# A transformer-like layer chain on one core: the routers' logits are formed inside both attentions, the norm of the routing moves to Pool and ACT

## The reference

```
x = x + conv(group_norm(x));  x = x + box3x3(group_norm(x))
t = tokens(x)                                   # 16 images x 256 tokens of 128 channels
t = t + softmax_attention(ln(t), 8 heads)       # image by image in the kernel
t = t + moe(ln(t), 8 experts, top 2, width 256)     # "d"
t = t + linear_attention(ln(t), 8 heads)
t = t + moe(ln(t), 8 experts, top 2, width 512)     # "f"

def moe(x):                                     # both layers
    logits = x @ router                         # 4096 tokens x 8 experts
    top2, index = top_k(logits, 2);  w = softmax(top2)
    y = sum over the two chosen experts of w * (silu(x @ g[e]) * (x @ u[e])) @ down[e]
```

## Time and profile before

| what | value |
| --- | --- |
| median of 3 runs | 883.47 us (879.12, 883.47, 885.61) |
| the profiled execution | 884.63 us, span in the trace 882.9 us |
| mean granted PE clock | .89 of full speed |
| busy in the span | PE 717.3 us (81%), DVE 521.0 (59%), ACT 416.2 (47%), POOL 401.1 (45%) |
| softmax_attention | to about 302.7 us |
| route d | 302.75 to 365 us |
| linear_attention | about 490 to 596.4 us |
| route f | 596.44 to 651.8 us |

### The profile page before, as it was taken

The page is one execution under the profiler, slowest core; times in us unless marked ns, Lnnn a source line. Parts: engine busy times, 40 slices in busy tenths (PEclk is TensorE's granted clock), DMA queues, the critical chain, the costliest instruction groups (busy, mean ns, idle before and its releaser), DMA issues. The chain is left out here.

```text
span 882.9 us, 17711 instructions
## 1 busy us (share of the span) xinstructions
PE 717.3 (81%) x5093; PEld 560.7 (64%) x5093; DVE 521.0 (59%) x1467; ACT 416.2 (47%) x1075; POOL 401.1 (45%) x436
## 2 busy tenths in 40 slices
PE   3996879899998762988999156568389999999996
PEld 1555656666665462757888145557268888888882
DVE  7447857777776358665555258885863333333334
ACT  2423436767675331565555255544244444444434
POOL 0003245556663033345664577700036676766740
PEclk9997969999998765699999688886569999999999
DMA  3001000000000051164333122205001111111118
GB/s 102 1 1 25 1 1 1 1 0 0 0 1 1 18 186 36 44 186 118 91 89 78 53 55 52 53 4 191 1 21 40 44 47 46 46 49 42 49 29 285
DMA packets 33974, 46.18 MB, mean 52 GB/s; under 512 B 8195, under 2 KB 22663, under 8 KB 33648
## 3 DMA queue, kind: packets, MB, share of 16 engines
q1 hardware_dynamic: 25040, 27.57, 9.8%
q0 software_dynamic: 8864, 17.72, 7.7%
HBM read 30.11 MB, written 15.60 MB: 52 GB/s over the span
## 5 line engine op out<-in xcount | busy, mean ns | idle before, releaser
L1986 DVE TENSOR_TENSOR f_h<-ps,f_silu 128x512 f32<-128x512 f32 x71 | 49.1, 692 | 121.5 <-ACT f_silu L1944 121.5
L1044 DVE TENSOR_REDUCE negmax<-ps 128x2 f32<-128x512 f32 x128 | 82.6, 687 | 44.3 <-PE ps L878 43.4
L1832 POOL DMA_INDIRECT f_xg<-f_normed,f_gather x71 | 68.9, 971 | 78.1 <-POOLq L1469 54.8
L1832 POOL DMA_INDIRECT d_xg<-d_normed,d_gather x71 | 67.6, 952 | 71.0 <-PE ps L1873 42.3
L1944 ACT ACTIVATE f_silu<-ps 128x512 f32<-128x512 f32 x71 | 42.4, 598 | 108.8 <-PE ps L1883 108.8
L1838 POOL DMA_INDIRECT f_results<-f_y,f_scatter x71 | 71.9, 1012 | 45.7 <-issue 32.0
L785 ACT ACTIVATE prob<-ps 128x512 f32<-128x512 f32 x128 | 69.6, 598 | 42.2 <-PE ps L897 42.1
L1262 POOL DMA_INDIRECT e_yg<-d_results,d_slot_u x64 | 61.5, 961 | 32.4 <-issue 18.6
L1904 PE MATMUL ps<-f_w_out,f_hT 128*128 x568 | 75.2, 276 | 0.6 <-DVE f_y L1992 0.6
L1904 PEld LDWEIGHTS ps<-f_w_out,f_hT 128*128 128x128 f32 x568 | 69.0, 192 | 0.9 <-issue 0.8
L1986 DVE TENSOR_TENSOR d_h<-ps,d_silu 128x256 f32<-128x256 f32 x71 | 30.0, 423 | 37.5 <-ACT d_silu L1944 36.7
(11 more groups left out here) (357 smaller groups left out, 1956.2 us busy)
## 6 DMA issues: line engine op xcount, KB each, us to landing
d_results<-d_y SPq DMA_DIRECT2D x71, 64.0 KB, 1.8
f_raw<-in_f_in SPq DMA_DIRECT2D x16, 256.0 KB, 3.0
f_ys<-f_results SPq DMA_DIRECT2D x8, 512.0 KB, 6.7
X<-in_x SPq DMA_DIRECT2D x4, 512.0 KB, 5.4
d_normed<-X SPq DMA_DIRECT2D x8, 256.0 KB, 2.0
d_raw<-in_d_in SPq DMA_DIRECT2D x8, 256.0 KB, 2.7
f_normed<-X SPq DMA_DIRECT2D x8, 256.0 KB, 2.0
f_w_out<-in_f_out SPq DMA_DIRECT2D x1, 2048.0 KB, 8.7
```

What stands on the lines that cost most here:

```text
L1044: nc.vector.tensor_reduce(negmax[:, :, h // HG, col:col + 1], ps[:, 2 + h % 2, :].rearrange("p (t k) -> p t k", t=2), AX_X, ALU.max, negat ...
L1832: nc.gpsimd.indirect_dma_start(xg[:, n % 4, :], None, moe.xn_dram, bass.IndirectOffsetOnAxis(ap=moe.gather[:, n:n + 1], axis=0)).then_inc( ...
L1986: nc.vector.tensor_tensor(h[:, n % 2, :], UP(n), silu[:, n % 2, :], ALU.mult).then_inc(h_ready, 1)
```

## The change

The logits of a normalised token are (t @ r - mean x sum(r)) / deviation. With a router whose column means are taken off, the mean falls out, and the factor 1/deviation doesn't change which experts are largest. So the logits are now formed from raw tokens with the centred router, and 1/deviation is applied only to the gap between the two chosen logits.

- `adaptive_conv` loads both routers, and PE forms the centring (`centre_routers`) and the products of the softmax attention's wo and bo with the router of d (`fold_routers`); DVE takes them out.
- In `softmax_attention` wv gets eight more columns (the centred router d) and wo eight more (wo times that router), so `project_v` and `output` write 136 columns instead of 128. ACT scales the eight columns of the input back by the deviation (`logits_in`, two small copies per image), and DVE's `add_output` adds the two parts (`top.logits`) in one more operation. The constant from bo is added in route d.
- In `linear_attention` PE transposes the tokens of image s-4 (`transpose_tokens`), ACT copies them, PE multiplies image s-5 by the centred router f (`token_logits`), ACT copies the logits. `transpose_tokens` stands first in PE's list and waits for `tok_ready`, which DVE's `add_tokens` raises. The pipelines of PE and ACT are written for a width of 2; PE's is unrolled.
- In both `route`s the router's load, PE's transposes and products, ACT's copies and DVE's normalise are gone. Pool works out mean and variance (eight operations on 128x32) ahead of its constants; ACT takes the root; DVE begins with the choice, works out `ln_rstd` and `ln_shift` between its two rounds, and then ACT normalises the even groups of tiles and Pool the odd ones, 16 tiles each. Pool's split of the weights in route d comes after its 16 tiles. SP issues the load of w_out and all raw pieces ahead of the stores of normalised tokens.

Setup lines, declarations and buffers are left out of the diff:

```diff
+                nc.tensor.matmul(CENTRE, average[:], raw_routers[:].rearrange("p l e -> p (l e)"),
...
+                nc.tensor.matmul(FOLD[:, 0:Moe.E], wo_T[:], top.routers[:, 0, :], start=True, stop=True)
+                nc.tensor.matmul(FOLD[:, Moe.E:], bo_wide[:], top.routers[:, 0, :], start=True,
+                                 stop=True).then_inc(fold_ps, 1)
...
                 nc.scalar.activation(vaug[:, b, :, :, 1:1 + HD],
-                                     V.rearrange("p (t h d) -> p t h d", t=2, d=HD), ACT.Copy).then_inc(v_ready, 1)
+                                     V[:, :, 0:C].rearrange("p t (h d) -> p t h d", d=HD), ACT.Copy)
+                for t in range(2):
+                    tile = bass.ds(2 * m + t, 1)
+                    last = nc.scalar.activation(top.logits_in[:, tile, :].rearrange("p t e -> p (t e)"), V[:, t, C:],
+                                                ACT.Copy, scale=top.ln_std[:, tile])
+                last.then_inc(v_ready, 1)
...
-                    last = nc.tensor.matmul(V[:, t * P:(t + 1) * P], xT[:, b, t * P:(t + 1) * P], wv[:],
+                    last = nc.tensor.matmul(V[:, t, :], xT[:, b, t * P:(t + 1) * P], wv[:],
...
                 dve.wait_ge(out_ps, n + 1)
                 dve.wait_ge(bo_added, n + 1)
-                t = T[:, bass.ds(2 * n, 2), :].rearrange("p t c -> p (t c)")
-                nc.vector.tensor_tensor(t, OUT, t, ALU.add).then_inc(tok_ready, 1)
+                tiles = bass.ds(2 * n, 2)
+                nc.vector.tensor_tensor(T[:, tiles, :], OUT[:, :, 0:C], T[:, tiles, :], ALU.add)
+                nc.vector.tensor_tensor(top.logits[:, tiles, :], OUT[:, :, C:], top.logits_in[:, tiles, :],
+                                        ALU.add).then_inc(tok_ready, 1)
...
-            pipeline(act, [(-1, transposed), (0, parts), (-2, normed), (-3, rstds)], N, 4)
+            act.sem_inc(logit_ps, 2)
+            def tokens_transposed(at, first, last):
+                act.wait_ge(tT_ps, at.n + 1)
+                act.wait_ge(logit_ps, at.n + 1)
+                nc.scalar.activation(tT[:, at.b, :], TT(at.b), ACT.Copy).then_inc(tT_ready, 1)
+            def logits(at, first, last):
+                act.wait_ge(logit_ps, at.n + 3)
+                nc.scalar.activation(top.logits[:, bass.ds(2 * at.n, 2), :].rearrange("p t e -> p (t e)"),
+                                     LOGITS(at.b), ACT.Copy).then_inc(logit_ready, 1)
+            pipeline(act, [(-1, transposed), (0, parts), (-2, normed), (-3, rstds), (5, logits),
+                           (4, tokens_transposed)], N, 2)
...
             def output(at, first, last):
                 pe.wait_ge(sum_ready, at.n + 3)
                 pe.wait_ge(heads_ready, at.n + 1)
+                pe.wait_ge(logit_ready, at.n + 1)
...
-            pipeline(pe, [(-1, transpose), (0, project), (2, output), (1, sum_tokens)], N, 2)
+            pe.sem_inc(tT_ready, 2)
+            pe.sem_inc(logit_ready, 4)
+            def transpose_tokens(at, first, last):
+                pe.wait_ge(tok_ready, at.n + 3)
+                pe.wait_ge(tT_ready, at.n + 1)
+                for t in range(2):
+                    ins = nc.tensor.transpose(TT(at.b)[:, t * P:(t + 1) * P],
+                                              T[:, bass.ds(2 * at.n + t, 1), :].rearrange("p t c -> p (t c)"), ident[:])
+                ins.then_inc(tT_ps, 1)
+            def token_logits(at, first, last):
+                pe.wait_ge(tT_ready, at.n + 3)
+                pe.wait_ge(logit_ready, at.n + 3)
+                for t in range(2):
+                    ins = nc.tensor.matmul(LOGITS(at.b)[:, t * Moe.E:(t + 1) * Moe.E], tT[:, at.b, t * P:(t + 1) * P],
+                                           top.routers[:, 1, :], start=True, stop=True)
+                ins.then_inc(logit_ps, 1)
+            pipeline(pe, [(4, transpose_tokens), (-1, transpose), (0, project), (2, output), (5, token_logits),
+                          (1, sum_tokens)], N, 2, True)
...
         @block.sync
...
-            sp.dma_start(router[:], router_dram).then_inc(router_in, 16)
-            groups = moe.xn_dram.rearrange("(p g t) c -> g p t c", p=P, t=GROUP)
-            for g in range(TILES // GROUP):
-                sp.wait_ge(xn_ready, g + 1)
-                sp.dma_start(groups[g], xn[:, g * GROUP:(g + 1) * GROUP, :]).then_inc(xn_stored, 16)
             sp.dma_start(moe.w_out[:], w_out_dram).then_inc(moe.weights_in, 16)
             if split is not None:
                 for i in range(split.pieces):
                     split.load(sp, i)
+            groups = moe.xn_dram.rearrange("(p g t) c -> g p t c", p=P, t=GROUP)
+            for g in range(TILES // GROUP):
+                sp.wait_ge((xn_even, xn_odd)[g % 2], g // 2 + 1)
+                sp.dma_start(groups[g], xn[:, g * GROUP:(g + 1) * GROUP, :]).then_inc(xn_stored, 16)
             sp.wait_ge(xn_stored, 16 * (TILES // GROUP))
...
         def _(pool):
             step = Chain(pool, chain_pool)
+            stats = top.ln_stats
+            difference, spread = moment[:, 0, :], moment[:, 1, :]
+            nc.gpsimd.tensor_tensor(spread, stats[:, :, 2], stats[:, :, 5], ALU.add)
+            nc.gpsimd.tensor_tensor(top.ln_mean[:], stats[:, :, 1], stats[:, :, 4], ALU.add)
+            step(nc.gpsimd.tensor_tensor(difference, stats[:, :, 1], stats[:, :, 4], ALU.subtract))
+            nc.gpsimd.tensor_scalar(spread, spread, 1.0 / C, None, ALU.mult)
+            nc.gpsimd.tensor_scalar(difference, difference, 0.5, None, ALU.mult)
+            step(nc.gpsimd.tensor_scalar(top.ln_mean[:], top.ln_mean[:], 0.5, None, ALU.mult))
+            step(nc.gpsimd.tensor_tensor(difference, difference, difference, ALU.mult))
+            nc.gpsimd.tensor_tensor(top.ln_std[:], spread, difference, ALU.add).then_inc(var_ready, 1)
             whole = dict(allow_small_or_imprecise_dtypes=True)
             nc.gpsimd.iota(up_to[:], pattern=[[1, P]], base=0, channel_multiplier=0, **whole)
             nc.gpsimd.iota(descending[:], pattern=[[-1, E]], base=E, channel_multiplier=0, **whole)
...
             nc.gpsimd.affine_select(out=before[:], in_=before[:], compare_op=ALU.is_ge, fill=0.0, base=-1,
                                     pattern=[[1, P]], channel_multiplier=-1).then_inc(consts_ready, 1)
+            pool.wait_ge(rstd_ready, 1)
+            for g in range(1, TILES // GROUP, 2):
+                for t in range(g * GROUP, (g + 1) * GROUP):
+                    ins = nc.gpsimd.tensor_scalar(xn[:, t, :], T[:, t, :], top.ln_mean[:, t:t + 1],
+                                                  top.ln_rstd[:, t:t + 1], ALU.subtract, ALU.mult)
+                ins.then_inc(xn_odd, 1)
             if split is not None:
...
         @block.scalar
         def _(act):
-            norm_on_scalar(act)
...
-            copy_logits(TILES // GROUP - 2, 0)
-            copy_logits(TILES // GROUP - 1, 1)
+            act.wait_ge(var_ready, 1)
+            nc.scalar.activation(top.ln_std[:], top.ln_std[:], ACT.Sqrt, bias=top.eps5[:]).then_inc(std_ready, 1)
+            act.wait_ge(shift_ready, 1)
+            for g in range(0, TILES // GROUP, 2):
+                for t in range(g * GROUP, (g + 1) * GROUP):
+                    ins = nc.scalar.activation(xn[:, t, :], T[:, t, :], ACT.Identity, bias=ln_shift[:, t:t + 1],
+                                               scale=top.ln_rstd[:, t:t + 1])
...
         @block.vector
         def _(dve):
             step = Chain(dve, chain)
-            norm_on_vector(dve)
...
-                        top.ln_mean[:, bass.ds(tile, 1)], top.ln_rstd[:, bass.ds(tile, 1)], ALU.subtract, ALU.mult)
-                    if t % GROUP == GROUP - 1:
-                        ins.then_inc(xn_ready, 1)
             dve.wait_ge(consts_ready, 1)
-            dve.wait_ge(logit_ready, TILES // GROUP + 2)
             by_tile = lambda ap: ap.unsqueeze(2).broadcast_to([P, TILES, E])
             by_expert = lambda ap: ap.unsqueeze(1).broadcast_to([P, TILES, E])
+            if constant is not None:
+                step(nc.vector.tensor_tensor(logits[:], logits[:], by_expert(constant[:]), ALU.add))
             for c, left in enumerate((logits, rest)):
...
                 step(nc.vector.tensor_tensor(chosen[:, c], by_expert(descending[:]), by_tile(rank[:]), ALU.is_equal))
                 if c == 0:
                     step(nc.vector.scalar_tensor_tensor(rest[:], chosen[:, 0], -1e30, logits[:], ALU.mult, ALU.add))
+                    dve.wait_ge(std_ready, 1)
+                    nc.vector.reciprocal(top.ln_rstd[:], top.ln_std[:]).then_inc(rstd_ready, 1)
+                    dve.wait_ge(rstd_ready, 1)
+                    nc.vector.scalar_tensor_tensor(ln_shift[:], top.ln_mean[:], -1.0, top.ln_rstd[:], ALU.mult,
+                                                   ALU.mult).then_inc(shift_ready, 1)
             nc.vector.tensor_tensor(both[:], chosen[:, 0], chosen[:, 1], ALU.add).then_inc(both_ready, 1)
```

(45 more changed lines are left out.)

122 lines of the change are left out of this document (62 added, 60 removed).

## The result

The changed kernel took 909.33 us (median of 4 runs, 899.89 to 912.23), the kernel before 884.38 (4 runs): a ratio of 1.0275, 95% interval 1.0185 to 1.0365. It is slower by about 25 us, where 15.5 were forecast; that it is slower is clear of the noise, that it is so by 2% or more is not. The profiled execution took 906.99 us with a span of 905.3, so 22.4 more than before.

The account below looks back on a forecast made before the run. PE was taken to bound softmax attention, the loop of waits linear attention. 884.63 - 25.0 (routes) + 1.8 (softmax attention, convolution) + 38.8 (linear attention) = 900.2 profiled, 899 as median; range 880 to 910.

Parts of the forecast that it names:

- Rival 3: Linear attention: wait covered if transposed tokens were added one DVE step earlier, a second step of lag; 865 us, chance .08.
- the sum of 8.7: Linear attention: length in us of the serial DVE-PE-ACT-DVE step with PE's burst at the lower clock level.
- the sum of 7.0: Linear attention: length in us of the same serial step, add to add, at full clock.
- The weight of two thirds: Linear attention: estimated share of PE bursts at the lower clock, giving 8.15 us steps and +26.3 over nine.
- The three short steps: Linear attention: three steps without gathered sums, 6.3 us each instead of 3.46, +8.5 (5.2 to 10.3).
- The tail: End of linear attention: further DVE, PE and ACT rounds for the last tokens, +4 us (3 to 6).
- Rival 2: Linear attention: every PE burst at half clock, +47.5 us, total 908; chance .19.
- Rival 1: Linear attention: PE's clock stays up, +24.1 us, total 884, no change; chance .20.
- Rival 4: Routes: POOL's tiles cost twice the upper bound or its statistics stall, half the gain; 911 us, chance .07.
- both bounds: Routes: a normalised tile on POOL estimated at 0.29 to 0.55 us, from two-scalar operations on 128x512.
- 43%: Routes: share of POOL's working time that DVE loses beside it, from 7.4 us over 17.1 of split in d.
- some 15 us of cover: Route d: POOL ends near 336, some 15 us before DVE's list, so SP's token stores would not be late.

Follow-up runs that it names:

- the order alone: Changed kernel with router products and token transposes moved to the end of PE's linear-attention step, two waits added, all work kept: 864.17 us.
- the wait alone: Changed kernel without the linear attention's token work but with PE's wait for DVE's add: 897.44 us; the same without that wait: 860.09 us.
- the fillers: Changed kernel with seven useless products of 256 columns at the end of each PE step of the linear attention: 888.88 us.

## Why the prediction was right, and where its sizes were off

**The linear attention's wait** was named with its place, its releaser and the reason why it can't be hidden, and all three are shown: by the order alone (864 against 909) and by the wait alone (897 against 860). Rival 3 decided as it was put: the distance between add and transpose is one step, and that is too little at the head of PE's list. At its end the same lag is enough, and the time is near the rival's 865. A second step of lag at the head, the rival's own condition, was not run.

**The length of the slow step was mis-sized.** The mechanism held, but not the sum of 8.7 for a burst at the lower level. Its head did: from the end of the add to the end of the k and v products pass 3.73 us (566.72 to 570.45), where its terms give 3.75. Two terms behind that were taken from a step at full clock, and they are too short. From ACT's k_exp to DVE's k feature 0.99 was forecast, and it is 1.67 (570.50 to 572.17): DVE makes the q feature first (L1509), which by the profile waited 4.52 us for PE's products of q (L1440), and these stand behind k and v in the burst. From there to the end of the add 3.85 was forecast, and it is 4.32 (572.17 to 576.49), with DVE idle for 0.42 until PE's sums were through. So at the lower level it is PE's whole burst (566.78 to 572.91) that closes the loop, and then DVE from its kv copy to the add (573.01 to 576.49): 0.06 + 6.13 + 0.10 + 3.48 = 9.77, and the step measured 9.76. DVE idles ahead of its kv copy in five of the nine steps, which last 8.61 to 9.90; the other four last 8.33 to 8.57.

For the full clock the sum of 7.0 was right: the fillers' step is 6.95, and the same two terms are 0.97 and 3.93 there. The weight of two thirds was near: (8.98 - 7.0) / (9.76 - 7.0) = 0.72, an estimate from these steps. So nine steps cost 33.8 instead of 26.3, above both ends (15.9 and 31.2). The three short steps came out as forecast in sum (+8.4 for +8.5), but partly by luck: they last 7.34, 6.67 and 4.78, and its ends were 5.2 and 6.9. The tail was 2 us longer.

**Rival 2** gave 908, and the time is 909, but not by its reason. Not every burst was slow: steps of 8.3 to 9.9 lie on both sides of its 8.7. That the range held the time is owed to this rival, since the forecast's own terms ended at 904. By the Trainium skill (TensorE: Matmul & The Clock Gate, HAM oscillation) a loop of short bursts with waits between, there for transfers, starts every round at the slow clock. The trace agrees in most rounds: in nine of the ten steps from the first add the token transposes that open the burst take 0.69, and 0.44 in one, after idle times of 3.62 us and more. Rival 1 had the clock stay up and is refuted: it fell to .71. Rival 4 (911) lies as near to the time as rival 2, but it is refuted as well: the routes gave all of their gain.

**The routes** gained 25.4 where 25.0 were forecast, by errors that cancel. The start of the choice was right (3.9 us with the constant, forecast 3.4 and 0.46, though the terms given for the 3.4 are 2.1 and 1.2). A tile on POOL costs 0.82, above both bounds (0.29 and 0.55), and that was named as a sign of being wrong: the rows of 512 elements were a poor measure for one of 128. But its share of DVE's time was far below 43%: in route f 13.1 us of tiles cost DVE 36.25 - 34.9 = 1.4 us, by the run with all tiles on ACT. The 43% came from the split, and there it nearly holds: without tiles on POOL the split costs DVE 42.0 - 34.9 = 7.1 of its 19.3 us beside the choice, or 37%; before it was 7.4 of 17.1. POOL was to end near 336 and ended at 347.25, because of the tiles and because the split, most of it beside the table loops, took 24.8 us instead of 18.6. Of some 15 us of cover for SP's stores 6 were left, which was enough: the first gather starts 1.1 behind the list (354.35). The open question of whether the table loops are held is answered: they are, by the split (2.29 for 1.22). The Trainium skill names contention for operations with two SBUF inputs (GPSIMD Engine Reference, 8. Key points), and the trace agrees. That section does not say which engine loses: beside the tiles the loops run on (1.21), and it is the tiles that take longer.

**Convolution and softmax attention** were priced at +1.8. The start of route d lies between 296.2 and 305.0 us in the traces of the changed kernels here, so this term can be neither confirmed nor refuted.

## What to carry to other kernels

In a software pipeline that semaphores hold together, a new stage needs not only a lag but a place: ask for each engine's list which instruction of which step the first wait looks at, and whether the waited-for engine needs what stands behind it. Put the stage with the latest input last in the step; here that alone made 909 into 864 us. When a loop becomes serial, work out the slow-clock step from slow-clock rows of every path, because another path can become the longest.

## What the runs showed of the hardware

More work on PE made a kernel faster: fillers of 51 us lifted the granted clock of the stretch from .71 to .98 and shortened it from 111.7 to 91.6 us.

POOL and DVE hold each other unequally. Beside DVE's two-input table comparisons a rounding copy (a cast to fp32r) and a subtraction of 128x512 on POOL took 1.60 and 1.66 us instead of 0.61 and about 1.3, and DVE's 1024-element comparison 2.29 instead of 1.22: both lose. A one-input operation with two scalars on 128x128 lets DVE's comparison run at 1.21 to 1.31 and takes 1.49 instead of 0.82 itself: nearly all of the loss is POOL's. Nor is one input a shelter for DVE: with all tiles on ACT its copy of 128x64 took 1.14 us beside the split in route d, and 0.20 in route f of the same trace, while its reductions of 128x256 kept their 0.42.
